# Adjacency GNN on one core: another order for the convolution taps, the second transposes and the opening's sums

## The chip, the cores and the metric

One core of a Trainium2 chip runs the kernel. The metric is the device time of one execution in microseconds (us). The kernel before has a median of 383.56 us over three runs (383.27 to 384.62).

## What is computed

The input is 32 graphs of 256 nodes with 128 features, and a 256 x 256 adjacency matrix for each. Two layers with a residual and a layer norm each:

```python
h = relu(bn1(conv1(x)));  x_conv = relu(bn2(conv2(h)) + x)          # conv2: 17 taps along the nodes
A = exp(-dist(x @ w_se)) * adj;  x_nmp = A @ relu(x @ w_msg)         # first product of a graph
y = GRU([x_conv, x_nmp], x);  x1 = layernorm(x + y)
h = (1 + eps) * x1 + adj @ x1                                        # second product of a graph
out = layernorm(x1 + relu(h @ W1 + b1) @ W2 + b2)
```

## The kernel before

The 32 graphs go in 8 groups of 4, a group in two pairs (index h). Every engine's instructions stand in an order written by hand in three functions: `prologue` (the opening, group 0's front part), `steady(s, u, front)` for the steps 1 to 7 and `last`. Steps 3 to 6 are a loop. In step s the back part of group s-1 (gates, first norm, product with the adjacency matrix, MLP, second norm) is interleaved with the middle part of group s (convolution, distances, product with A) and the front of group s+1 (`conv1`). Order between engines comes only from semaphores: each helper waits for the count of the stage that it reads and raises that of the stage that it writes. A wait holds up everything queued behind it on its engine.

The 17-tap convolution is done at seven points (HALF, ZERO, PLUS2, MINUS2, PLUS1, MINUS1, INF): input sums per point (`sv`), a short convolution of 4 or 5 taps on PE (L1367 in plain float32, L1314 as three products of high and low parts), and sums of the outputs on DVE into `usum` (L972 `u_sum`, L982 `pair2_sum`, L990 and L991 `pair2_add`, L995 `pair1_sum`, L1003 `pair1_add`, L1008 `inf_add`). High parts (`xh`, `sth`, `wh`, `nmph`) are rounded on ACT, low parts (`xl`, `stl`, `wl`, `nmpl`) are differences on DVE (L860, L1106). The weights' low parts are made in step 1 (`tap_low`) and the taps of each point in the opening (L1150).

Names that the change and the prediction touch:
- PE: `plain_taps`/`taps` (one point), `y_transpose(gb, h)` (L1479), `distances` (L1420), `aggregate` (the product with the adjacency matrix, L1428 into `back`), `nmp` (the product with A, L1428 into `front`), `mlp1`, `mlp2` (L1523), `conv1`.
- DVE: `y_stats` (L1044, L1048) and `y_apply` (L1066): first norm of a pair, with the root on POOL between them. `x_low` (L860, `xl`), `h_low` (L860, `nmpl` from `back`), `out_stats` (L1079, L1044, L1048): starts when `mlp2` is done.
- POOL: `rsqrt` (L543), `mask` (L564, `amat`, four in a step), `add_b2` (L558), `add_diagonal` (L577), and in step 1 alone `x_low1` (L569), which makes the low part of group 1's x.
- ACT: `h1_out` (L665), `minus2_out` (L678), `minus1_out` (L685), `exps` (L694).

A group counts two low parts of x on one semaphore, and group 1's are POOL's. So `x_low` has a wait for group 2 alone:

```python
if isinstance(g, int) and g == 2:
    wait(dve, XL_READY, 1, 2)
```

## Time and profile before

| | |
|---|---|
| median of three runs | 383.56 us (383.27 to 384.62) |
| the profiled execution | 383.36 us, of which 381.6 us are its span |
| busy PE, DVE, ACT, POOL | 95%, 85%, 61%, 56% of the span |
| granted TensorE clock | 0.996 on average |
| one loop step | 44.0 us, eight groups |

The span is the time between the first and the last instruction of the profiled execution. A row of the timeline gives the start and the duration in us, the engine, the line of the kernel, the operation, what it writes from what it reads, the count of merged instructions, and in brackets how long the engine had been idle and what ended that. The same tile name stands for all of its buffers.

### The profile page before, as it was taken

Reading aid. Unit: us, or ns where it says so; the run is one execution under the profiler, and the core shown is the slowest. Engines: PE = TensorE matmul, PEld = TensorE weight load, DVE = VectorE, ACT = ScalarE, POOL = GpSimd, SP = SyncE. Lnnn points to the kernel's source line nnn. Section 1 sums busy time; section 2 is a strip of 40 time slices with the busy share of each in tenths; the row PEclk is TensorE's granted clock in tenths of the full one; section 3 lists DMA queues with packets and bytes.
Section 4 is the critical chain, followed back from the end, with each engine's and each line's share of the span. In section 5 each row is a group of like instructions: output and inputs, shape, how many; then the busy total and the mean of one; then the engine's idle time right before and its main releaser. Section 6 shows DMA issues by size and latency. Waiting matters only on the chain.

```text
span 381.6 us, 6424 instructions
## 1 busy us (share of the span) xinstructions
PE 363.7 (95%) x2150; PEld 315.6 (83%) x2150; DVE 323.0 (85%) x674; ACT 232.3 (61%) x436; POOL 215.0 (56%) x190
## 2 busy tenths in 40 slices
PE   7998998899999999999999999999999999999994
PEld 4776778599898888989888998989888998988973
DVE  4999989998699986999689986999779986995584
ACT  3463665555767376673875657674676648555765
POOL 3135344946349753697437863497536973296362
PEclk9999999999999999999999999999999999999998
DMA  5700004200013010130110300130101301000002
GB/s 196 267 3 0 0 3 165 83 29 28 29 55 112 0 58 1 55 112 2 56 33 26 108 27 29 55 110 0 55 0 55 110 2 55 3 1 2 0 29 82
DMA packets 8135, 19.39 MB, mean 51 GB/s; under 512 B 688, under 2 KB 5168, under 8 KB 7088
## 3 DMA queue, kind: packets, MB, share of 16 engines
q1 hardware_dynamic: 7536, 18.17, 13.9%
q10 hardware_dynamic: 576, 0.92, 0.7%
q8 instruction: 13, 0.21, 0.2%
q14 instruction: 10, 0.08, 0.1%
HBM read 14.90 MB, written 4.19 MB: 50 GB/s over the span
## 4 chain that ended last, share of the span: by engine, by line
PE 60%; DVE 27%; issue 5%; ACT 2%; POOL 2%; DMA 2%; SPq 0%; DVEq 0%; ACTq 0%; POOLq 0%
PE back L1314 24%; PE conv L1314 16%; PE back L1428 5%; PE back L1523 3%; DVE stats L1044 3%; PE conv L1367 3%; DVE stl L860 3%; PE front L1400 2%; PE front L1428 2%; DVE tail L1079 2%; POOL rstd L543 2%; DMA xv<-in_x_dram 2%; DVE xn L1066 2%; DVE nmpl L860 1%; DVE wl L1106 1%
## 5 line engine op out<-in xcount | busy, mean ns | idle before, releaser
L1314 PE MATMUL conv<-sth,wh 128*128 128x256 f32 x207 | 62.4, 301 | 2.8 <-DVE stl L860 2.2
L1314 PE MATMUL conv<-sth,wl 128*128 128x256 f32 x207 | 58.9, 285 | 0.0
L1314 PE MATMUL conv<-stl,wh 128*128 128x256 f32 x207 | 58.8, 284 | 0.0
L543 POOL TENSOR_TENSOR rstd<-rstd,small 128x4 f32<-128x4 f32 (+1 forms) x34 | 38.3, 1127 | 34.2 <-DVE rstd L1048 33.7
L564 POOL TENSOR_TENSOR amat<-amat,adjT 128x512 f32<-128x512 f32 x32 | 49.4, 1576 | 9.6 <-ACT amat L694 9.6
L548 POOL TENSOR_TENSOR xw<-xw,xv 128x512 f32<-128x512 f32 (+1 forms) x17 | 21.7, 1279 | 48.0 <-ACT xw L718 48.0
L1314 PEld LDWEIGHTS conv<-sth,wh 128*128 128x128 f32 x207 | 39.0, 189 | 5.4 <-issue 1.6
L1314 PEld LDWEIGHTS conv<-stl,wh 128*128 128x128 f32 x207 | 39.0, 189 | 0.1
L1314 PEld LDWEIGHTS conv<-sth,wl 128*128 128x128 f32 x207 | 39.0, 189 | 0.0
L650 ACT ACTIVATE sth<-sv 128x272 fp32r<-128x272 f32 (+1 forms) x33 | 17.2, 522 | 34.2 <-DVE sv L888 22.2
L577 POOL TENSOR_TENSOR adjT<-adjT,diag 128x256 f32<-128x256 f32 x32 | 28.4, 916 | 6.1 <-DVE msg L934 6.1
L735 ACT ACTIVATE tail<-tail,shift,rstd 128x128 f32<-128x128 f32 x60 | 24.1, 481 | 11.2 <-DVE shift L1101 11.2
L1428 PE MATMUL front<-amat,msg 128*128 128x256 f32 x128 | 29.1, 379 | 0.0
L1428 PE MATMUL back<-adjT,xn 128*128 128x256 f32 x120 | 28.2, 387 | 0.8 <-DVE xn L1066 0.8
L558 POOL TENSOR_TENSOR tail<-xn,later_w 128x512 f32<-128x512 f32 x15 | 27.3, 1823 | 1.8 <-DVE xn L1066 1.4
L742 ACT ACTIVATE tail<-back,first_w 128x512 f32<-128x512 f32 (+1 forms) x30 | 20.4, 683 | 11.4 <-PE back L1314 11.4
L1523 PEld LDWEIGHTS back<-later_w,tail 128*128 128x128 f32 x224 | 26.2, 192 | 0.6
L1523 PE MATMUL back<-later_w,tail 128*128 128x128 f32 x224 | 26.3, 275 | 0.0
L1428 PEld LDWEIGHTS back<-adjT,xn 128*128 128x128 f32 x120 | 22.0, 190 | 5.2 <-DVE xn L1066 1.5
L1428 PEld LDWEIGHTS front<-amat,msg 128*128 128x128 f32 x128 | 23.8, 190 | 2.9
L528 POOL TENSOR_TENSOR sv<-vv 128x272 f32<-128x272 f32 x7 | 8.3, 1187 | 30.3 <-DVE vv L915 30.3
L1003 DVE TENSOR_TENSOR usum<-usum,pm 128x512 f32<-128x512 f32 x16 | 23.7, 1518 | 0.1
(240 smaller groups left out, 1036.4 us busy)
## 6 DMA issues: line engine op xcount, KB each, us to landing
adjT<-in_adj_dram SPq DMA_DIRECT2D x8, 1024.0 KB, 4.9
out_dram<-tail SPq DMA_DIRECT2D x15, 256.0 KB, 2.2
xv<-in_x_dram SPq DMA_DIRECT2D x7, 512.0 KB, 3.3
tail<-in_conv_dram ACTq DMA_DIRECT2D x3, 256.0 KB, 4.5
gbuf<-in_gates_dram SPq DMA_DIRECT2D x1, 576.0 KB, 8.2
xv<-in_x_dram SPq DMA_DIRECT2D x2, 256.0 KB, 5.3
tail<-in_conv_dram SPq DMA_DIRECT2D x1, 320.0 KB, 5.0
later_w<-in_later_dram SPq DMA_DIRECT2D x1, 320.0 KB, 5.3
```

The source lines that it names most:

```text
L543: done(pool.tensor_tensor(rstd[:, k, v, q], rstd[:, k, v, q], minus_half[:, q], ALU.pow), RSTD[k])
L548: done(pool.tensor_tensor(xw[:, h, part(c)], xw[:, h, part(c)], xv[u][:, part_cols(h, c)], ALU.mult), XWX_READY)
L558: done(pool.tensor_tensor(out_tile(h, c)[:, q, :], xn[:, h, q, :], b2bc.unsqueeze(1).to_broadcast([P, len(part_blocks(c)), D]), ALU.add), ...
L564: done(pool.tensor_tensor(amat[:, b, :, :], amat[:, b, :, :], adjT[u][:, b, :, :], ALU.mult), A_READY)
L577: done(pool.tensor_tensor(dg, dg, diag[:, :].unsqueeze(1).to_broadcast([P, PAR, P]), ALU.add), ADJE_READY)
L650: done(act.activation(dst, src, ACT.Copy), name)
L735: last = act.activation(o[:, q, :], o[:, q, :], ACT.Identity, bias=shift[:, v, q:q + 1], scale=rstd[:, 1, v, q:q + 1])
L742: done(act.activation(hid[:, h, f, part(c)], bank("hid", h, c, f), ACT.Relu, bias=vec[:, B1 + f:B1 + f + 1]), HID_READY)
L1003: done(dve.tensor_tensor(a, a, p1, ALU.add), PRE_READY)
L1314: ins = pe.matmul(bank, a, b, start=first and k == 0, stop=last and k == len(todo) - 1)
L1428: ins = pe.matmul(tile[:, k * N:(k + 1) * N], lhs(b, rm), rhs(b, rm), start=rm == 0, stop=rm == PAR - 1)
L1523: ins = pe.matmul(tile[:, k * P:(k + 1) * P], hid[:, h, f, q * P:(q + 1) * P], w2[:, f, :], start=f == 0, stop=f == 1)
```

## The change

Only orders change, no instruction is added or removed. The opening: on ACT `h1_out` of group 0 goes ahead of the second high part of x, and `minus2_out(0)` ahead of two of the exponentials. On DVE `u_sum(0)` and `pair2_sum(0)` go ahead of the stream and the taps at -1, and the low part of x goes behind the output sums. On PE the product `nmp(0, 0)` goes ahead of the taps at -1. On POOL the first two `add_diagonal` wait for `inf_add` and no longer for a rounded product. In the steps: on PE the taps at -1 stand directly behind those at 1, the second `y_transpose` behind them with the distances, and INF ahead of both `aggregate`. In step 1 `mlp2(gb, 0)` goes ahead of `conv1`. DVE follows: `pair2_sum` and the low part of INF's stream ahead of the second `y_stats`, one `x_low` ahead of the second `y_apply` and one behind it, and `pair2_add` behind both `h_low`.

```diff
--- before.py
+++ after.py
@@ -595,7 +595,7 @@
                 streams2(1)
                 pool.wait_ge(mlp_loaded, 16)
                 pool.wait_ge(diag_ready, 1)
-                wait(pool, NH_READY, 0, 1)
+                wait(pool, PRE_READY, 0, 3)
                 add_diagonal(0, 0, 0)
                 add_diagonal(0, 0, 1)
                 wait(pool, MSUM_READY, 1, 1)
@@ -755,12 +755,12 @@
                 act.activation(wh[:, 0, :], c1raw, ACT.Copy).then_inc(w_high, 1)
                 act.wait_ge(x_pair0_loaded, 16)
                 high(xh[0][:, cols(0)], xv[0][:, cols(0)], XH_READY)
-                wait(act, X_LOADED, 0, 16)
-                high(xh[0][:, cols(1)], xv[0][:, cols(1)], XH_READY)
                 act.wait_ge(pads_zeroed, 1)
                 act.wait_ge(bn_ready, 1)
                 h1_out(0, 0)
                 h1_out(0, 1)
+                wait(act, X_LOADED, 0, 16)
+                high(xh[0][:, cols(1)], xv[0][:, cols(1)], XH_READY)
                 act.wait_ge(conv2_loaded, 64)
                 x_high(1, 1)
                 for k in range(3):
@@ -774,11 +774,11 @@
                 h1_out(1, 0, True)
                 exps(0, 0)
                 exps(0, 1)
-                h1_out(1, 1, True)
+                act.wait_ge(bn_ready, 3)
+                minus2_out(0)
                 exps(0, 2)
                 exps(0, 3)
-                act.wait_ge(bn_ready, 3)
-                minus2_out(0)
+                h1_out(1, 1, True)
                 act.wait_ge(tap_sums, 11)
                 tap_high(PLUS1)
                 minus1_out(0)
@@ -1175,12 +1175,12 @@
                 taps_step(even, w0, 1.0, w2)
                 taps_step(minus1, w1, 1.0, w3)
                 taps_step(plus1, even, 1.0, minus1)
+                dve.wait_ge(tap_sums, steps[0])
+                u_sum(0, 0)
+                pair2_sum(0)
                 first_stream1(MINUS1, ALU.subtract)
                 taps_step(minus1, minus1, -1.0, even)
                 dve.wait_ge(tap_sums, steps[0])
-                u_sum(0, 0)
-                x_low(0, 0, 1)
-                pair2_sum(0)
                 first_diffs(1)
                 half_stream(1)
                 zero_stream(1)
@@ -1191,9 +1191,10 @@
                 pair1_add(0, 1)
                 inf_add(0)
                 nmp_low(0, 0)
+                nmp_low(0, 1)
                 xconv_low(0, 0)
-                nmp_low(0, 1)
                 w_low_part(wl[:, S_GATE:S_GATE + 9, :], graw, wh[:, S_GATE:S_GATE + 9, :], w_count("gates"))
+                x_low(0, 0, 1)
                 tap_low(PLUS1)
                 xconv_low(0, 1)
 
@@ -1207,16 +1208,15 @@
                 if first:
                     stream_low(gm, 2)
                 reset(gb, 0)
+                add_input(gb, 0)
                 if first:
                     tap_low(MINUS2)
-                add_input(gb, 0)
                 gates_end(gb, 0)
                 stream_low(gm, 3)
                 if first:
                     tap_low(ZERO)
                     reset(gb, 1)
                     tap_low(MINUS1)
-                    inf_stream(gm)
                 else:
                     inf_stream(gm)
                     u_sum(gm, u)
@@ -1224,28 +1224,31 @@
                 add_input(gb, 1)
                 y_stats(gb, 0)
                 gates_end(gb, 1)
+                if first:
+                    inf_stream(gm)
                 y_apply(gb, 0)
-                y_stats(gb, 1)
                 pair2_sum(gm)
-                y_apply(gb, 1)
-                stream_low(gm, 4)
                 if first:
                     tap_low(INF)
+                stream_low(gm, 4)
+                y_stats(gb, 1)
+                if front:
+                    x_low(gf, 1 - u, 0)
+                y_apply(gb, 1)
+                if first:
                     w_low_part(w1l[:, :], w1raw, w1h[:, :], w_count("w1"))
                     h_low(gb, 0)
                     u_sum(gm, u)
+                    h_low(gb, 1)
+                    pair1_sum(gm)
+                    x_low(gf, 1 - u, 1)
                 else:
-                    pair2_add(gm)
+                    if front:
+                        x_low(gf, 1 - u, 1)
                     h_low(gb, 0)
                     pair1_sum(gm)
-                h_low(gb, 1)
-                if first:
-                    pair1_sum(gm)
-                if front:
-                    x_low(gf, 1 - u, 0)
-                    x_low(gf, 1 - u, 1)
-                if first:
-                    pair2_add(gm)
+                    h_low(gb, 1)
+                pair2_add(gm)
                 pair1_add(gm, 0)
                 pair1_add(gm, 1)
                 if second:
@@ -1551,8 +1554,8 @@
                 for b in range(GB):
                     distances(0, b)
                 plain_taps(0, PLUS1)
+                nmp(0, 0)
                 plain_taps(0, MINUS1)
-                nmp(0, 0)
                 plain_taps(1, HALF)
                 nmp(0, 1)
                 plain_taps(1, ZERO)
@@ -1580,28 +1583,31 @@
                     pe.wait_ge(w_low, w_count(MINUS2))
                 taps(gm, MINUS2)
                 taps(gm, PLUS1)
-                y_transpose(gb, 1)
                 if first:
                     pe.wait_ge(w_low, w_count(MINUS1))
                 taps(gm, MINUS1)
+                y_transpose(gb, 1)
                 distances(gm, 0)
                 distances(gm, 1)
+                if first:
+                    pe.wait_ge(w_low, w_count(INF))
+                taps(gm, INF)
                 aggregate(gb, ub, 0)
                 aggregate(gb, ub, 1)
                 distances(gm, 2)
                 distances(gm, 3)
                 if first:
-                    pe.wait_ge(w_low, w_count(INF))
-                taps(gm, INF)
-                if first:
                     pe.wait_ge(w_low, w_count("w1"))
                     pe.wait_ge(mlp_loaded, 16)
                 mlp1(gb, 0)
                 mlp1(gb, 1)
+                if first:
+                    mlp2(gb, 0)
                 if front:
                     conv1(gf, ub, 0)
                     conv1(gf, ub, 1)
-                mlp2(gb, 0)
+                if not first:
+                    mlp2(gb, 0)
                 if front:
                     mlp2(gb, 1)
                 nmp(gm, 0)
```

DVE in the opening, from the taps at 1 to the first instruction of group 1 (L972, L976: `u_sum`; L982: `pair2_sum`; L882 and the last L1150: stream and taps at -1; `xl`: `x_low`; L875: `first_diffs(1)`):

```order
 L1150 SCALAR_TENSOR_TENSOR gbuf<-adjT 128x640
+L972 SCALAR_TENSOR_TENSOR usum<-conv,first_w,xv 128x4x64 x4
+L976 SCALAR_TENSOR_TENSOR usum<-conv,first_w,usum 128x4x64
+L982 SCALAR_TENSOR_TENSOR pm<-conv,first_w,pm 128x4x64 x2
 L882 TENSOR_TENSOR sv<-vv 128x272
 L1150 SCALAR_TENSOR_TENSOR adjT<-adjT 128x640
-L972 SCALAR_TENSOR_TENSOR usum<-conv,first_w,xv 128x4x64 x4
-L976 SCALAR_TENSOR_TENSOR usum<-conv,first_w,usum 128x4x64
-L860 TENSOR_TENSOR xl<-xv,xh 128x512
-L982 SCALAR_TENSOR_TENSOR pm<-conv,first_w,pm 128x4x64 x2
 L875 TENSOR_TENSOR av<-h 128x4x2x68
```

The output sums now run before the stream and the taps at -1, and `x_low` has left this stretch.

DVE in step 1 with the changed order, from `tap_low(INF)` through the second pair's norm (the waits stand in brackets; `xl_ready` counts the low parts of x, `rstd1_ready` the roots of the first norm):

```order
L1106 TENSOR_TENSOR wl<-tail,wh 128x512 [waits w_high]
L860 TENSOR_TENSOR stl<-sv,sth 128x272 [waits streams_high_ready]
L1044 BN_STATS stats<-back 128x6 [waits y_full]
L1044 BN_STATS stats<-back 128x6
L1048 TENSOR_SCALAR rstd<-stats 128x4 [waits stats1_ready]
L860 TENSOR_TENSOR xl<-xv,xh 128x512 [waits xl_ready,xh_ready]
L1066 TENSOR_SCALAR xn<-back,stats,rstd 128x128 [waits rstd1_ready]
L1066 TENSOR_SCALAR xn<-back,stats,rstd 128x128 x3
L1106 TENSOR_TENSOR w1l<-later_w,w1h 128x256 [waits w_high]
```

Before, both `xl` instructions stood behind `pair1_sum`, well behind `w1l`. Now the first stands between the statistics (L1048) and the normalisation (L1066) of the second pair.

DVE in step 2, from the second pair's statistics to `pair1_add` (the loop steps read the same), before:

```order
L1048 TENSOR_SCALAR rstd<-stats 128x4
L982 SCALAR_TENSOR_TENSOR pm<-conv,first_w,pm 128x4x64 x2
L1066 TENSOR_SCALAR xn<-back,stats,rstd 128x128 x4
L860 TENSOR_TENSOR stl<-sv,sth 128x272
L990 TENSOR_TENSOR usum<-usum,pm 128x512
L991 SCALAR_TENSOR_TENSOR usum<-pm,usum 128x512
L860 TENSOR_TENSOR nmpl<-back,nmph 128x512
L995 SCALAR_TENSOR_TENSOR pm<-conv,first_w,pm 128x512
L860 TENSOR_TENSOR nmpl<-back,nmph 128x512
L860 TENSOR_TENSOR xl<-xv,xh 128x512 x2
L1003 TENSOR_TENSOR usum<-usum,pm 128x4x128 x2
```

and with the change:

```order
L1048 TENSOR_SCALAR rstd<-stats 128x4
L860 TENSOR_TENSOR xl<-xv,xh 128x512
L1066 TENSOR_SCALAR xn<-back,stats,rstd 128x128 x4
L860 TENSOR_TENSOR xl<-xv,xh 128x512
L860 TENSOR_TENSOR nmpl<-back,nmph 128x512
L995 SCALAR_TENSOR_TENSOR pm<-conv,first_w,pm 128x512
L860 TENSOR_TENSOR nmpl<-back,nmph 128x512
L990 TENSOR_TENSOR usum<-usum,pm 128x512
L991 SCALAR_TENSOR_TENSOR usum<-pm,usum 128x512
L1003 TENSOR_TENSOR usum<-usum,pm 128x4x128 x2
```

The two `x_low` have moved forward, and `pair2_add` (L990, L991) has taken their place directly ahead of `pair1_add` (L1003).

## Rows read from the trace of the kernel before

**Rows 1.** Windows by stage: length, busy us (count) of PE, PEld, DVE, ACT, POOL.
```profile
0.00:45.35 45.35, 39.25 (x172) 30.26 (x173) 38.66 (x78) 22.34 (x41) 14.73 (x24) 1.00 0.29 98
45.35:89.90 44.55, 41.58 (x238) 35.17 (x237) 42.00 (x83) 24.97 (x45) 27.36 (x23) 1.00 0.16 60
89.90:135.63 45.73, 44.34 (x269) 38.79 (x267) 40.49 (x83) 28.53 (x54) 28.71 (x23) 1.00 0.14 47
...
179.65:223.75 44.10, 43.83 (x271) 38.92 (x272) 38.33 (x80) 28.33 (x53) 27.44 (x23) 1.00 0.14 49
```

**Rows 2.** Timeline of PE, opening and step 1, rows with idle time before them.
```profile
34.81 2.44 PE L1367 MATMUL conv<-sv,first_w 128*128 128x256 f32 x10 [1.51 <-DVE sv L888]
...
41.39 2.41 PE L1367 MATMUL conv<-sv,first_w 128*128 128x256 f32 x10 [0.68 <-issue]
...
63.94 0.63 PE L1479 MATMUL back<-ident_w,gbuf 128*128 128x128 f32 x4 [1.06 <-DVE gbuf L1037]
...
76.40 0.47 PE L1314 MATMUL back<-nmph,w1h 128*128 128x512 f32 x1 [0.93 <-DVE nmpl L860]
```

**Rows 3.** Timeline of DVE in the opening.
```profile
27.13 1.89 DVE L1150 SCALAR_TENSOR_TENSOR adjT<-adjT 128x640 f32<-128x640 f32 x1
...
31.02 0.92 DVE L860 TENSOR_TENSOR xl<-xv,xh 128x512 fp32r<-128x512 f32 x1
...
38.40 2.29 DVE L1003 TENSOR_TENSOR usum<-usum,pm 128x512 f32<-128x512 f32 x2
```

**Rows 4.** Timeline of POOL in the opening.
```profile
25.52 5.87 POOL L564 TENSOR_TENSOR amat<-amat,adjT 128x512 f32<-128x512 f32 x4 [9.60 <-ACT amat L694]
...
38.29 1.85 POOL L577 TENSOR_TENSOR adjT<-adjT,diag 128x256 f32<-128x256 f32 x2
```

**Rows 5.** Timeline of DVE in step 1.
```profile
65.98 0.17 DVE L1048 TENSOR_SCALAR rstd<-stats 128x4 f32<-128x4 f32 x1
...
67.27 1.37 DVE L1066 TENSOR_SCALAR xn<-back,stats,rstd 128x128 f32<-128x128 f32 x4 [0.34 <-POOL rstd L543]
...
71.60 1.50 DVE L1106 TENSOR_TENSOR w1l<-later_w,w1h 128x256 fp32r<-128x256 f32 x1
...
79.42 1.29 DVE L1003 TENSOR_TENSOR usum<-usum,pm 128x512 f32<-128x512 f32 x2
```

**Rows 6.** Timeline of POOL in step 1.
```profile
66.23 1.01 POOL L543 TENSOR_TENSOR rstd<-rstd,small 128x4 f32<-128x4 f32 x1 [1.10 <-DVE rstd L1048]
67.20 1.28 POOL L569 TENSOR_TENSOR xl<-xv,xh 128x512 fp32r<-128x512 f32 x1
...
80.86 1.34 POOL L519 TENSOR_TENSOR av<-h 128x544 f32<-128x544 f32 x1 [4.12 <-ACT h L665]
```

**Rows 7.** Timeline of DVE in a loop step, from 205 us.
```profile
205.00 0.68 DVE L990 TENSOR_TENSOR usum<-usum,pm 128x512 f32<-128x512 f32 x1
...
208.17 2.76 DVE L860 TENSOR_TENSOR xl<-xv,xh 128x512 fp32r<-128x512 f32 x2
210.86 3.47 DVE L1003 TENSOR_TENSOR usum<-usum,pm 128x512 f32<-128x512 f32 x2
214.98 0.69 DVE L1079 TENSOR_TENSOR tail<-back,tail 128x512 f32<-128x512 f32 x1 [0.66 <-PE back L1523]
```

**Rows 8.** Timeline of POOL in the same loop step.
```profile
204.82 2.62 POOL L558 TENSOR_TENSOR tail<-xn,later_w 128x512 f32<-128x512 f32 x1 [0.24 <-DVE xn L1066]
207.38 6.40 POOL L564 TENSOR_TENSOR amat<-amat,adjT 128x512 f32<-128x512 f32 x4
```

**Rows 9.** Timeline of PE in the same loop step and at its end.
```profile
200.75 0.37 PE L1314 MATMUL conv<-sth,wh 128*128 128x256 f32 x1
200.96 0.28 PE L1314 MATMUL conv<-stl,wh 128*128 128x256 f32 x1
201.07 0.28 PE L1314 MATMUL conv<-sth,wl 128*128 128x256 f32 x1
...
223.75 0.38 PE L1314 MATMUL conv<-sth,wh 128*128 128x256 f32 x1 [0.27 <-DVE stl L860]
```

## The prediction

> **What bounds the kernel now.** I read the windows by stage first [rows 1]. In a loop step PE is busy 43.83 of 44.10 us, in the opening 39.25 of 45.35, in step 1 41.58 of 44.55, in step 2 44.34 of 45.73. A stage here ends where PE begins the taps at 2, except the opening, which ends where the gates begin. So an order of work can win at most 6.1 us in the opening, 3.0 in step 1, 1.4 in step 2 and 0.3 in each of the four loop steps. DVE has 38 to 42 busy us in the same windows and is the second bound.
>
> The timeline of PE then shows who ends the idle time [rows 2]: DVE's half stream of group 1 (1.51 us at 34.81), `inf_add` on DVE (0.68 at 41.39, which the view calls issue; the taps at 2 of group 1 wait for it), the second gate output ahead of the second `y_transpose` in step 1 (1.06 at 63.94), the second `h_low` (0.93 at 76.40). At the end of a loop step it is a low part of a stream (0.27 at 223.75, [rows 9]). All of these are DVE's. So DVE is read next, beside POOL.
>
> **DVE and POOL hold each other up.** `pair1_add` takes 1.29 us for two instructions where POOL is idle [rows 5], 2.29 beside `add_diagonal` [rows 3, 4] and 3.47 beside four masks [rows 7, 8]. So an instruction of 0.65 waits for about one POOL instruction. The reverse is seen too: `add_b2` takes 2.62 us where DVE runs `pair2_add` beside it, and `pair2_add` keeps its 0.68 [rows 7, 8]. Which of two waits is decided by who comes first.
>
> **The opening: -1.7 us.** The low part of x (0.92) leaves DVE's way to group 1's streams [rows 3]. The first two `add_diagonal` now start behind `inf_add`, so `pair1_add` should cost 1.29 instead of 2.29, 1.0 less [rows 3, 4, 5]. Against that, the taps at -1 (1.89 under a mask [rows 3]) now stand behind `u_sum` and `pair2_sum`: done at 29.0 before, they are done when the masks let them, which run from 25.52 to 31.39 [rows 4]. The taps' 640 elements take some 0.8 us by `pair1_add`'s 0.65 for 512, just ahead of the last mask's end or behind it: 31.0 to 32.2, 31.7 taken. PE uses the gap for `nmp(0, 0)`, and from 31.7 it has work without a hole: the taps at -1 (ten instructions like the half stream's, 2.2 us) and what it did from 34.81 to 45.35 less 0.68 idle, 9.8 us [rows 1, 2]. The gates would start at 43.7 instead of 45.35: -1.7. At best all 2.5 us of PE's idle time after 29 go away, at worst only `x_low`'s 0.9. The earlier `h1_out` costs and brings nothing: DVE wins some tenths by it, which end in the same wait for the masks.
>
> **Step 1: +1.6 us.** The second `y_transpose` no longer leaves 1.06 of idle time in front of it. But the new order has a wait that the diff doesn't show as such: `x_low` of group 2 waits for POOL's low part of group 1, and now stands between the second pair's statistics and its normalisation. POOL does the root first (1.01), then that low part (1.28), and only then may DVE go on [rows 6]. Before, the statistics ended at 66.15 and the normalisation began at 67.27, 1.12 later [rows 5]. Now: 1.01 + 1.28 + two handovers of 0.05 + `x_low` itself 0.65 = 3.0, so 1.9 us more on DVE, and 3.2 if POOL's next instruction, `add_b2`, gets in ahead of `x_low` (2.62 less the 1.3 of `pair2_add` [rows 7, 8]). DVE's work up to the second `h_low` is the end of PE's idle time at 76.40, so the delay goes to PE. What gives it back in part is `w1l`, which waits for less POOL work (1.50 before [rows 5], 0.4 at best). There is a second brake: `mlp2(0, 0)` goes ahead of `conv1`, which moves `h1_out` and POOL's `token_diffs` of group 2 (80.86, [rows 6]) about 1.8 us back against the MLP, and DVE's streams of group 2 need them. Bounds of what is given back: 0.7 (`w1l` and half of the wait hidden) to 2.7. I take 1.6, nearly all that the opening wins, because both brakes act on the same stretch.
>
> **Step 2: +0.65 us, the loop steps: +0.6 us together.** PE has the same work, so only what DVE finishes late counts. It counts from `out_stats`, which starts when `mlp2` ends (214.98) after 0.66 of idle time [rows 7]. The second `h_low` ended at 208.17 [rows 7]; INF's twelve instructions now lie ahead of the second `aggregate`, 12 x 0.12 [rows 9] = 1.5 us, so it ends at 209.7. Behind it stand four instructions of 0.65 that read and write SBUF: `pair2_add` has changed places with the two `x_low`. The masks: 6.40 us less three waits of 0.6 are 1.15 each [rows 8]; they begin at about 208.1, because `add_b2` comes 1.5 later and is held up less. Alternating, DVE's four end at 215.3, or at 214.7 if the phase is kinder: 0 to 0.3 us late, 0.15 taken, over four loop steps 0.6. If each waits longest, 0.6 per step. In step 2 two weights' low parts follow `pair1_add` and the idle time is gone already (1.4 us of PE idle time, [rows 1]), so all of the later end counts: 0.65, between 0 and 1.2. Step 7 has no `x_low` and no wait at its end: nothing.
>
> **PE's changes of kind: -0.6 us.** The first tap behind a `y_transpose` takes 0.21 us to the next one, the second 0.11 [rows 9]. The taps at -1 behind those at 1 save that 0.09, seven times. At most twice that, if the `distances` behind it save as much, at least nothing: no row shows `distances` behind a transpose.
>
> **The sum.** -1.7 + 1.6 + 0.65 + 0.6 - 0.6 = +0.55 on the profiled execution's 383.36 us: 383.9. The median of the runs is 0.2 above it, so I say 384.0 us. Against the median that is +0.1%; 0.5%, 1.9 us, is about what can be told from no change. The ends added up: -2.5 + 0.7 - 1.2 gives 380.4, -0.9 + 2.7 + 1.2 + 2.4 gives 388.8.
>
> **Rivals.** First, **the opening's gain stays**: POOL's low part is done by the time DVE asks, or DVE catches up because it has fewer waits. For it: DVE's idle 0.34 ahead of the normalisation goes [rows 5], and step 1 loses the 1.06 [rows 2]. Against it: POOL's low part stands behind a root that needs the very statistics ahead of `x_low`. Time: 383.36 - 1.7 - 1.06 - 0.6 = 380.0. Chance 0.15.
>
> Second, **the masks hold DVE in every step**: all four instructions behind the second `h_low` wait for POOL, and `out_stats` starts late. It decides where `pair1_add` ends more than 0.66 us later than before [rows 7]; from there every tenth is one of PE's. With 3.47 / 2 = 1.74 for each of the four [rows 7], from 209.7 to 216.7, less one that finds POOL done (1.1) and half of another: 215.9 to 216, 0.9 late. Four loop steps 3.6, step 2 1.4, the rest as forecast (-1.7 + 1.6 - 0.6): +4.3, so 387.7. Chance 0.24. For it: `pair2_add` never ran beside masks in a step before. Against it: the first two masks now run while DVE waits for `h_low`. The Trainium skill (SBUF — State Buffer, section "SBUF: two separate sides") has it that a DVE instruction with two SBUF inputs and a GpSimd instruction that reads SBUF exclude each other for a whole instruction, the first one there winning. By that rule moving two such instructions under the masks costs what this rival says; the 2.62 and the 3.47 agree with it.
>
> Third, that **the change doesn't do what it says**, since PE is without a hole in the loop and its groups only change places: then only the opening and step 1 speak, between 382.7 (-1.7 + 1.6 - 0.6) and 384.4 (-1.7 + 2.7). That lies within the forecast's case, which has 0.61.
>
> **How the numbers follow.** Forecast 0.61, nearly all of it within 0.5%. Faster by over 0.5% (under 381.6): most of the first rival, 0.14. Slower (over 385.5): the second and the forecast's upper tail, 0.25. Same 0.61. The range from 381.0 to 387.2 cuts the outer part of either rival, a tenth at each end.
>
> **What would show it.** Right: the gates start at 43 to 44.5 us; DVE idles 1 us or more ahead of `xl` in step 1, ended by POOL's L569; the second `h_low` of step 1 is about where it was; `pair2_add` takes 1 to 1.8 us for an instruction; PE's gap ahead of the taps at 2 in the loop is 0.2 to 0.6. Wrong: no idle time ahead of that `xl`, and step 2 beginning 2 us or more earlier (first rival); loop steps of over 44.6 us (second); or an opening that isn't shorter, because the taps at -1 come later than 32.2.

## The result and the profile after

The changed kernel takes 394.3 us (median of 6 runs, 392.87 to 395.28), the kernel before 383.5 (6 runs, 383.27 to 384.62): a ratio of 1.028, 95% interval 1.0264 to 1.0296. It is slower by 10.8 us where 0.5 was forecast, and the time lies above the range. The profiled execution has a span of 392.4 us against 381.6.

The windows by stage of the kernel after, cut as in [rows 1] (the opening ends where the gates begin, every step where PE begins the taps at 2; then length, busy us and count of PE, PEld, DVE, ACT, POOL, and the granted clock):

```profile
0.00:43.14 43.14, 38.87 (x172) 30.40 (x173) 36.76 (x77) 22.25 (x41) 13.64 (x24) 1.00 0.30 103
43.14:91.32 48.18, 43.99 (x239) 37.16 (x237) 43.35 (x83) 24.11 (x45) 26.26 (x23) 0.93 0.15 56
91.32:139.36 48.04, 44.67 (x266) 38.73 (x267) 41.95 (x83) 28.60 (x54) 28.05 (x24) 1.00 0.12 44
...
184.22:229.14 44.92, 44.24 (x271) 38.70 (x272) 38.04 (x80) 28.09 (x53) 26.85 (x23) 1.00 0.15 48
...
318.88:392.40 73.52, 65.01 (x393) 56.89 (x393) 50.53 (x118) 42.84 (x85) 33.72 (x34) 0.96 0.07 22
```

The opening is 2.2 us shorter than in [rows 1]. Step 1 is 3.6 longer, step 2 2.3, a loop step 0.8, and the stretch from step 7 to the end takes 73.5 us where it took 69.8 (311.78 to 381.6). The loss is in every step, and in step 1 (0.93, before 1.00) and at the end (0.96, before 0.98) the clock column is lower too.

**Step 1.** PE in the kernel after, by its timeline (start, length, engine, line, operation, idle time before it):

```profile
66.29 0.55 PE L1317 MATMUL conv<-sth,wh 128*128 128x256 f32 x1 [3.18 <-DVE stl L860]
66.64 0.41 PE L1317 MATMUL conv<-stl,wh 128*128 128x256 f32 x1
66.86 0.41 PE L1317 MATMUL conv<-sth,wl 128*128 128x256 f32 x1
...
68.99 5.51 PE L1431 MATMUL back<-adjT,xn 128*128 128x256 f32 x16
```

And DVE in the same stretch:

```profile
65.17 0.67 DVE L1106 TENSOR_TENSOR wl<-tail,wh 128x512 fp32r<-128x512 f32 x1
65.77 0.42 DVE L860 TENSOR_TENSOR stl<-sv,sth 128x272 fp32r<-128x272 f32 x1
...
69.50 1.67 DVE L860 TENSOR_TENSOR xl<-xv,xh 128x512 fp32r<-128x512 f32 x1 [2.43 <-POOL xl L569]
```

The wait that the prediction expected is there: `x_low` stands 2.43 us and takes 1.67, and the normalisation begins 2.9 us later behind the statistics than before (71.09 - 67.07 against 1.12, [rows 5]), near the worse of its two cases. But PE shows a larger hole that it did not expect: 3.18 us ahead of INF, ended by the stream's low part (65.77), which DVE reaches only behind `pair2_sum` and INF's weight (65.17). And behind the hole PE runs slowly. A tap followed the one before by 0.11 us in [rows 9] and follows by 0.22 here, and the two aggregates (16 matmuls) take 5.51 us, where they took 3.94 in the kernel before. The windows behind the hole show the clock that was granted:

```profile
66.20:69.00 2.80, 2.71 (x13) 2.74 (x14) 0.84 (x3) 1.53 (x4) 1.85 (x2) 0.50 0.00 0
69.00:72.00 3.00, 3.00 (x9) 2.35 (x8) 2.50 (x4) 0.00 (x0) 1.62 (x2) 0.50 0.00 0
72.00:75.00 3.00, 2.89 (x15) 1.87 (x14) 2.72 (x8) 1.06 (x2) 2.47 (x2) 0.99 0.00 0
```

0.50 is the lower of the two levels, 1.2 GHz. It was granted from the hole's end to about 72 us.

**A loop step.** DVE of the kernel after, by the timeline:

```profile
208.34 0.69 DVE L860 TENSOR_TENSOR xl<-xv,xh 128x512 fp32r<-128x512 f32 x1
209.93 1.37 DVE L1066 TENSOR_SCALAR xn<-back,stats,rstd 128x128 f32<-128x128 f32 x4 [0.90 <-POOL rstd L543]
...
214.62 1.44 DVE L990 TENSOR_TENSOR usum<-usum,pm 128x512 f32<-128x512 f32 x1
215.99 1.77 DVE L991 SCALAR_TENSOR_TENSOR usum<-pm,usum 128x512 f32<-128x512 f32 x1
217.86 2.18 DVE L1003 TENSOR_TENSOR usum<-usum,pm 128x512 f32<-128x512 f32 x2
219.97 0.68 DVE L1079 TENSOR_TENSOR tail<-back,tail 128x512 f32<-128x512 f32 x1
...
221.48 1.09 DVE L1048 TENSOR_SCALAR rstd<-stats 128x4 f32<-128x4 f32 x1
```

POOL beside it:

```profile
208.48 1.42 POOL L543 TENSOR_TENSOR rstd<-rstd,small 128x4 f32<-128x4 f32 x1 [3.93 <-DVE rstd L1048]
...
212.99 5.90 POOL L564 TENSOR_TENSOR amat<-amat,adjT 128x512 f32<-128x512 f32 x4
219.49 1.76 POOL L519 TENSOR_TENSOR av<-h 128x544 f32<-128x544 f32 x1 [0.59 <-ACT h L665]
221.21 1.33 POOL L521 TENSOR_TENSOR av<-h 128x544 f32<-128x544 f32 x1
```

And the load of PE's weights for the second aggregate:

```profile
211.35 1.59 PEld L1431 LDWEIGHTS back<-adjT,xn 128*128 128x128 f32 x8 [0.53 <-DVE xn L1066]
```

`pair2_add` (L990, L991) now takes 1.44 and 1.77 us beside the masks, where it took 0.68 each [rows 7]: what the second rival described. `pair1_add` ends 35.8 us after the taps at 2 began (220.04 - 184.22), in the kernel before 34.7 (214.33 - 179.65, [rows 7]), and the 0.66 of idle time ahead of `out_stats` is gone. Two more things are late, though. The second normalisation ends 27.1 us after the taps at 2 (211.30 - 184.22), before it was 25.1, and in spite of INF in front of it the second aggregate waits 0.53 us. And the variance of `out_stats` (L1048, a 128x4 instruction) takes 1.09 us beside POOL's `token_diffs`, in the kernel before 0.68. Which of the three sets the step, one profile doesn't tell. The experiments go into it, and the rows of all of them together give an answer (below, "What all runs share").

**Step 7 and the last group.** PE ahead of the last gates:

```profile
358.23 0.47 PE L1317 MATMUL back<-xh,wh 128*128 128x512 f32 x1 [2.00 <-DVE nmpl L860]
```

The windows around them:

```profile
358.00:360.00 2.00, 1.77 (x5) 1.46 (x6) 1.30 (x3) 0.00 (x0) 2.00 (x4) 0.69 0.04 8
360.00:362.00 2.00, 2.00 (x6) 1.60 (x5) 0.00 (x0) 0.03 (x1) 1.35 (x2) 0.50 0.00 0
```

The gates wait 2.00 us for `nmp_low`, which stands behind `pair2_add`, `pair1_add`, `inf_add` and `out_stats` on DVE. Then they run at 0.50 again, up to about 362 us. The prediction had put this stage at nothing.

### The profile page after: what moved, and what is told of

Read it like the earlier page. It is cut to its first block, busy times and chain, and to the rows that moved or that the text cites. A ratio compares the mean times of both kernels' runs of the same rounds, so it can differ in the third digit from the quotient of the medians.

```text
span 392.4 us, 6424 instructions
## 1 busy us (share of the span) xinstructions
PE 369.1 (94%) x2150; PEld 318.2 (81%) x2150; DVE 324.1 (83%) x674; ACT 230.6 (59%) x436; POOL 208.4 (53%) x190
## 4 chain that ended last, share of the span: by engine, by line
DVE 37%; PE 34%; issue 15%; POOL 5%; ACT 4%; DMA 2%; SPq 0%; DVEq 0%; ACTq 0%; POOLq 0%
PE back L1317 14%; PE conv L1317 6%; PE back L1431 4%; POOL rstd L543 4%; DVE stats L1044 4%; PE conv L1370 3%; DVE stl L860 3%; DVE usum L991 3%; DVE xn L1066 3%; DMA xv<-in_x_dram 2%; DVE gbuf L1029 2%; DVE usum L990 2%; PE front L1403 2%; DVE wl L1106 2%; DVE tail L1079 2%
## 5 line engine op out<-in xcount | busy, mean ns | idle before, releaser
L543 POOL TENSOR_TENSOR rstd<-rstd,small 128x4 f32<-128x4 f32 (+1 forms) x34 | 39.9, 1174 | 50.5 <-DVE rstd L1048 50.1
L564 POOL TENSOR_TENSOR amat<-amat,adjT 128x512 f32<-128x512 f32 x32 | 46.1, 1472 | 9.8 <-ACT amat L694 9.8
L1431 PE MATMUL back<-adjT,xn 128*128 128x256 f32 x120 | 30.4, 400 | 1.6 <-DVE xn L1066 1.2
L1431 PE MATMUL front<-amat,msg 128*128 128x256 f32 x128 | 29.1, 379 | 0.0
L1431 PEld LDWEIGHTS back<-adjT,xn 128*128 128x128 f32 x120 | 22.8, 199 | 7.3 <-DVE xn L1066 3.3
L650 ACT ACTIVATE nmph<-back 128x512 fp32r<-128x512 f32 (+1 forms) x16 | 9.2, 572 | 29.5 <-PE back L1431 29.5
L1066 DVE TENSOR_SCALAR xn<-back,stats,rstd 128x128 f32<-128x128 f32 x60 | 20.5, 403 | 6.3 <-POOL rstd L543 5.6
L558 POOL TENSOR_TENSOR tail<-xn,later_w 128x512 f32<-128x512 f32 x15 | 21.0, 1402 | 3.7 <-DVE xn L1066 3.4
```

The costliest lines, as they stand in the source:

```text
L543: done(pool.tensor_tensor(rstd[:, k, v, q], rstd[:, k, v, q], minus_half[:, q], ALU.pow), RSTD[k])
L558: done(pool.tensor_tensor(out_tile(h, c)[:, q, :], xn[:, h, q, :], b2bc.unsqueeze(1).to_broadcast([P, len(part_blocks(c)), D]), ALU.add), ...
L564: done(pool.tensor_tensor(amat[:, b, :, :], amat[:, b, :, :], adjT[u][:, b, :, :], ALU.mult), A_READY)
L650: done(act.activation(dst, src, ACT.Copy), name)
L1066: last = dve.tensor_scalar(xn[:, h, q, :], src(q, q + 1), stats[:, 0, v, q, 1:2], rstd[:, 0, v, q:q + 1], ALU.subtract, ALU.mult)
L1431: ins = pe.matmul(tile[:, k * N:(k + 1) * N], lhs(b, rm), rhs(b, rm), start=rm == 0, stop=rm == PAR - 1)
```

## The experiments

All were compared with the kernel before on the same chip. The table is worked out from the timelines: a step runs from the first `messages` instruction of its group on PE to that of the next group, and the last column but one from that of step 7 to the end of the span. Steps 3 to 6 are a mean. The steps are those of the profiled execution, and they add up to its span; the time, a median, is 0.2 to 2.9 us above that span.

```
kernel                     to step 1  step 1  step 2  3 to 6   end    time
before                       43.64    48.43   45.49   44.04   67.9   383.5
after                        41.43    52.13   47.73   44.88   71.6   394.3
e3 opening alone             41.08    49.29   45.48   44.05   67.8   382.5
e4 steps alone               44.01    51.66   48.31   44.88   70.0   395.1
e1 pair2_add back            42.47    52.00   46.25   45.05   68.9   390.8
e2 INF back                  42.71    54.90   46.40   45.97   70.1   399.2
e5 x_low behind norm.        41.27    52.28   47.83   44.94   71.7   394.6
e6 DVE's old tail            41.95    52.17   47.84   44.95   68.9   392.4
e7 mlp2 back in step 1       41.16    51.43   47.77   44.88   71.6   393.4
e8 transposes back           41.55    53.60   47.88   44.47   71.5   394.4
e9 transposes alone          41.55    49.27   47.08   45.55   69.4   391.6
e10 step 1 as before         43.10    49.28   47.74   44.88   71.6   391.5
e11 opening, late nmp_low    41.38    49.28   45.05   43.65   67.8   380.2
e12 INF between aggregates   42.55    53.60   48.31   44.88   70.0   395.2
e13 e8 and e1 together       41.38    51.92   45.80   44.59   68.6   389.0
e14 remainder, late nmp_low  41.14    49.31   45.38   44.21   68.6   383.4
e15 e13, masks first         41.26    52.69   48.99   49.38   69.1   411.3
```

The column "to step 1" also holds how soon the first work of all starts (9.1 to 10.9 us from run to run). Without that it is 34.1 us in the kernel before and e4, which have the old opening, and 32.0 to 32.4 in all others.

### The two halves of the change

e3 takes the opening's part of the diff into the kernel before; e4 takes the same part out of the kernel after.

> The kernel before with the change's opening alone (POOL's wait, ACT's, DVE's and PE's prologues). Theory: the opening's 2.2 us (gates at 43.14 instead of 45.35) is a gain of its own that step 1 passes on: 383.5 - 2.2 = 381.3 us. Rival (step 1 gives it back, because its streams' low parts and weights are ready no earlier and x of group 1 or its weights' low parts hold PE): 382.5 to 383.5 us.

382.48 us against 383.33, ratio 0.998 (0.9969 to 0.9992). In the profile the messages of step 1 start 2.6 us earlier, 0.5 of which is an earlier start of the first work (9.08 against 9.56). Step 1 gives 0.9 back: PE waits 0.57 us there for a gate's output of ACT's (at 55.43), and later for the same low parts as before. That leaves 1.2, and the times say 0.85: a small gain, and the rival's numbers (382.5 to 383.5) rather than the theory's 381.3.

> The changed kernel with the opening of the kernel before: the changes of the steps alone. Theory: the two parts add up, 394.3 + 2.2 = 396.5 us, with step 1 at 48 us, steps 3 to 6 at 44.9 and PE's gaps of 3 us in step 1 and 2 us ahead of the last gates. Rival (step 1's loss is the opening's gain given back, since DVE's list up to INF's stream takes equally long whenever the gates begin): 394 to 395 us, step 1 at 46 us.

395.08 us: 0.8 more than the kernel after, not 2.2. The loss is in the steps. Step 1 takes 51.66 us behind the old opening too, so its loss isn't the opening's gain given back. The halves don't simply add up: the end of e4 takes 1.6 us less than that of the kernel after, with a clock that stays at 1.00 there (last section).

### Step 1

e10 gives step 1 the lists of the kernel before on DVE and PE and leaves the other steps as changed.

> The changed kernel with the order of the kernel before on DVE and PE in step 1 alone (opening and steps 2 to 7 as changed). Theory (step 1's loss is its own: INF ahead of the aggregates waits 3.18 us for its stream's low part, PE's clock is granted at half behind that gap, and the aggregates wait for x_low's late normalisation): step 1 takes 49.3 us from messages to messages as in the kernel with the opening alone (52.1 in the changed kernel), PE's clock is 1.00 there: 394.3 - 2.8 = 391.5 us. Rival (part of it comes back in step 2, whose DVE is full as well): 392.5 to 393.5 us.

Step 1 is 49.28 us, as with the opening alone, and 391.48 in all: 2.8 us of the loss belong to step 1's order, and step 2 takes none of it over (47.74). Which part of that order is it? e5 moves the first `x_low`:

```diff
                 y_stats(gb, 1)
-                if front:
-                    x_low(gf, 1 - u, 0)
                 y_apply(gb, 1)
...
                     pair1_sum(gm)
+                    x_low(gf, 1 - u, 0)
                     x_low(gf, 1 - u, 1)
...
```

The lines shown at the end are those of step 1. In steps 2 to 7 it goes directly behind `y_apply`.

> The changed kernel with the first x_low taken out from between the second pair's statistics and its normalisation (behind the normalisation in steps 2 to 7, behind pair1_sum in step 1); nothing else. Theory X (x_low in that place holds the normalisation, by itself in step 1, and in the loop by slowing POOL's root beside it from 1.02 to 1.42 us): in steps 3 to 6 the root is 1.02 us again, the second aggregate no longer waits (0.53 us before), and a step takes 44.4 to 44.6 instead of 44.9 us; in step 1 the 2.43 us of idle time ahead of xl and the 1.67 of xl itself go from DVE's way, and step 1 is 1.5 to 2.5 us shorter. Together 394.3 - 1.6 - 2 = 390.5 us. Rival (the pair2_add behind the h_lows is what sets out_stats, and step 1 waits for the streams of group 2): the loop stays at 44.9, step 1 gains less than 0.7 us, about 393.5 us.

394.57 us, step 1 at 52.28 and the loop at 44.94: nothing, in either. The wait is gone and nothing is won, because DVE now idles in front of the first `h_low` instead. The timeline of DVE in e5:

```profile
69.32 1.43 DVE L1106 TENSOR_TENSOR w1l<-later_w,w1h 128x256 fp32r<-128x256 f32 x1
73.05 0.69 DVE L860 TENSOR_TENSOR nmpl<-back,nmph 128x512 fp32r<-128x512 f32 x1 [2.30 <-ACT nmph L650]
```

The aggregate that this `h_low` reads runs at half clock (16 matmuls in 5.28 us) and is what comes last. So the wait that the prediction had costed stood beside one that it had not seen, and taking away the first alone brings nothing. e2 takes the hidden part from the other side: INF goes behind both aggregates, as before.

```diff
-                if first:
-                    pe.wait_ge(w_low, w_count(INF))
-                taps(gm, INF)
                 aggregate(gb, ub, 0)
                 aggregate(gb, ub, 1)
                 distances(gm, 2)
                 distances(gm, 3)
+                if first:
+                    pe.wait_ge(w_low, w_count(INF))
+                taps(gm, INF)
```

> The changed kernel with INF put back behind both aggregates on PE in every step; DVE's order as changed. Theory A (pair2_add's place alone costs): the four instructions behind the second h_low still alternate with the masks, and as both the h_lows and the masks come 1.5 us earlier, out_stats is late no more than before: it recovers in this kernel as well, 44.0 to 44.3 us in steps 3 to 6; then lateness is the sum of two moves and either alone is free. Theory B (INF's place costs): the same in the loop. They part in step 1: there INF waits for its stream's low part, which was the 3.18 us gap at 66.29; behind the aggregates that gap should be gone and step 1 fall from 48.2 to about 45.5, unless x_low's wait of 2.43 us on DVE only moves it to the MLP (46.5). All together 394.3 - 3 (loop) - 2 (step 2) - 2 (step 1) - 2 (step 7) = 385 us; if pair2_add's place costs by itself, the loop steps stay at 44.6 or more and the time at about 390.

399.21 us, the opposite of what I had expected, in the loop too. PE's timeline of e2, in step 1:

```profile
73.78 3.56 PE L1431 MATMUL back<-adjT,xn 128*128 128x256 f32 x8 [5.96 <-DVE xn L1066]
```

and in a loop step:

```profile
215.21 1.99 PE L1431 MATMUL back<-adjT,xn 128*128 128x256 f32 x8 [1.60 <-DVE xn L1066]
```

Without INF in front, the second aggregate waits 5.96 us for the normalisation in step 1 and 1.6 in each loop step. So in the loop INF ahead of the aggregates is a cover: it hides a normalisation that the rest of the change has made late. e12 tries the middle, INF between the aggregates:

```diff
                 aggregate(gb, ub, 0)
+                if first:
+                    pe.wait_ge(w_low, w_count(INF))
+                taps(gm, INF)
                 aggregate(gb, ub, 1)
```

> The changed kernel with INF between the two aggregates of every step instead of ahead of both. Theory (in step 1 the gap of 3.18 us in front of INF and the half clock behind it cost most of the 3 us; in the loop it is DVE that is late, in whatever order PE goes): in step 1 the first aggregate runs in the gap, INF waits at most 1.3 us, the granted clock stays at 1.00, and step 1 takes 49.5 to 50.5 us from messages to messages instead of 52.1; the loop stays at 44.8 to 45: 394.3 - 2 = 392.3 us. Rival (the half clock is no matter, x_low's wait of 2.43 us on DVE then holds the second aggregate): step 1 at 51.5 to 52.5, 394 us.

395.22 us. The loop is the same to 0.01 us, and step 1 is 1.5 us longer. There the hole moves to the second aggregate, by PE's timeline of e12:

```profile
73.61 3.67 PE L1431 MATMUL back<-adjT,xn 128*128 128x256 f32 x8 [4.46 <-DVE xn L1066]
```

and by its windows the clock falls behind this hole:

```profile
72.00:75.00 3.00, 1.40 (x3) 1.17 (x4) 3.00 (x9) 0.00 (x0) 1.37 (x2) 0.77 0.00 0
75.00:78.00 3.00, 3.00 (x12) 1.96 (x11) 1.50 (x5) 0.69 (x2) 2.47 (x3) 0.66 0.00 0
```

So the run doesn't price the half clock by itself; e8 and e13 below do. e7 undoes the "second brake":

```diff
-                if first:
-                    mlp2(gb, 0)
...
-                if not first:
-                    mlp2(gb, 0)
+                mlp2(gb, 0)
```

> The changed kernel with mlp2 of the first pair behind conv1 in step 1 as well, as before. Theory (second brake: mlp2 ahead of conv1 delays ACT's h1_out of group 2, POOL's token_diffs and with it the half stream by up to 1.9 us): PE's conv1, h1_out and token_diffs come 1 to 1.5 us earlier and step 1 ends 0.8 to 1.5 us earlier: 393 us. Rival (out_stats, which waits for that mlp2, stands ahead of the half stream on DVE and moves back as far): no gain, 394 to 395 us.

393.42 us, step 1 at 51.43: 0.7 us, a little under the expectation. That brake is real.

### The loop

e1 is the test of the second rival:

```diff
                         x_low(gf, 1 - u, 1)
+                    pair2_add(gm)
                     h_low(gb, 0)
                     pair1_sum(gm)
                     h_low(gb, 1)
-                pair2_add(gm)
+                if first:
+                    pair2_add(gm)
```

> The changed kernel with pair2_add put back ahead of the two h_lows in steps 2 to 7 (step 1 as changed). Theory A (the place of pair2_add is what costs: it stands behind the second h_low and alternates with the masks): of the +10.8 us of the changed kernel's profile, steps 3 to 6 lose their +0.83 each (44.0 to 44.2 us again), step 2 its excess of 2.3, and step 7 with the last group its 3.7, since inf_add and both nmp_low come 2 us or more earlier and PE's gap of 2.00 us ahead of the last gates goes, with the half clock behind it; step 1 stays at 48.2. About 394.3 - 3.3 - 2.0 - 3.4 = 385.6 us. Theory B (INF ahead of the aggregates moves everything behind it, whatever DVE's order): the steps stay at 44.6 to 44.9, about 392 us. Theory C (DVE pays ahead of the h_lows instead): pair2_add beside add_b2 delays the first h_low, PE waits in front of mlp1, 388 to 390 us.

390.77 us (ratio 1.0191, 1.0174 to 1.0208). Theory A holds for step 2 (46.25, 1.5 us less) and for the end (68.9, 2.7 less), and falls for the loop: 45.05 us, no better. There DVE now waits 2.29 us ahead of `out_stats`, and the step is no shorter. By POOL's rows the second `add_b2` now stands beside `pair2_add` and takes 2.87 us (1.65 in the kernel after), the masks end 1.2 us later in the step, and `token_diffs` starts only when they end. e6 gives DVE its old tail in steps 2 to 7 (in step 1 both `x_low` go behind `pair1_sum`):

```diff
                 y_stats(gb, 1)
-                if front:
-                    x_low(gf, 1 - u, 0)
                 y_apply(gb, 1)
...
-                    if front:
-                        x_low(gf, 1 - u, 1)
+                    pair2_add(gm)
                     h_low(gb, 0)
                     pair1_sum(gm)
                     h_low(gb, 1)
+                    if front:
+                        x_low(gf, 1 - u, 0)
+                        x_low(gf, 1 - u, 1)
...
```

> DVE's order of the kernel before from the normalisation on in steps 2 to 7 (pair2_add ahead of the h_lows, both x_low behind them), in step 1 the two x_low behind pair1_sum; the rest of the changed kernel. If x_low's place and pair2_add's place are each a cost, this is the sum: the loop at 44.1 to 44.3 us, step 2 at 46, the last group without its gap of 2 us, step 1 at 46: 383.5 + 2 = 385.5 us. If what costs in the loop is INF ahead of the aggregates with its stream's low part ahead of the second pair's statistics, whatever stands behind them, the loop stays at 44.7 or more, about 388 us.

392.43 us, the loop at 44.95, the second of the two cases. PE is on time there (`mlp1` begins 29.1 us after the taps at 2, 214.04 - 184.95, before 29.2), and the step is no shorter. In the timeline of DVE in e6 the masks hold `x_low` and `pair1_add` up to `out_stats`, because the second `h_low` ends 30.0 us after the taps at 2, where it was 28.5 in [rows 7]:

```profile
214.96 2.50 DVE L860 TENSOR_TENSOR xl<-xv,xh 128x512 fp32r<-128x512 f32 x2
217.38 3.47 DVE L1003 TENSOR_TENSOR usum<-usum,pm 128x512 f32<-128x512 f32 x2
220.77 0.68 DVE L1079 TENSOR_TENSOR tail<-back,tail 128x512 f32<-128x512 f32 x1
```

POOL's `token_diffs` starts directly behind the masks, and with those adds of DVE's beside it the first takes 1.79 us instead of 1.34, by POOL's timeline of e6:

```profile
220.25 1.79 POOL L519 TENSOR_TENSOR av<-h 128x544 f32<-128x544 f32 x1
```

e8 puts the second transposes back ahead of the taps at -1, and e9 makes that one move alone, on top of the opening:

```diff
                 taps(gm, PLUS1)
+                y_transpose(gb, 1)
...
                 taps(gm, MINUS1)
-                y_transpose(gb, 1)
```

> The changed kernel with the second y_transpose of every step back ahead of the taps at -1. Theory (the second transposes set the chain statistics, root, normalisation, second aggregate, which the loop waits for): the statistics of the second pair start 0.35 us earlier (DVE is free then), the wait of the second aggregate falls from 0.53 to 0.2, a loop step takes 44.5 to 44.6 instead of 44.9, and 0.1 per step comes back for the taps' first instruction: 392.5 to 393.5 us; in step 1 PE waits about 1 us in front of the second y_transpose again, and the gap of 3.18 us ahead of INF is 1 us shorter. Rival (the transposes' place is harmless): 394.3 to 395 us, the loop at 44.9 or 45.

394.44 us. The loop gets its 0.4 us (44.47). Step 1 takes 1.5 us more, but not by this move: e13 below has the same order in step 1 and takes 51.92 there. In both, PE is without work for 1.88 us ahead of INF, and the second aggregate begins with the normalisation, 31.1 us after the messages. In e8 it then runs at the lower clock (0.50 from 73 to 76 us, 8 matmuls in 3.64 us). In e13 the lower clock came earlier (0.56 from 67 to 70), ahead of that wait, and the same 8 take 1.99. So here the half clock by itself costs 1.7 us, or nothing where a wait hides it.

> The kernel before with the change's opening, and of the steps' changes only one: the second y_transpose of every step behind the taps at -1. Theory M (the moves hold each other up: the late transposes need INF ahead of the aggregates as a cover, INF needs its stream's low part early, and that delays the second pair's statistics): alone, the transposes make the normalisation of the second pair 1.5 us later and the second aggregate waits about 1.2 us for it; the h_lows and the masks come later, and a loop step takes 45 us or more against 44.05 in the kernel with the opening alone: 382.5 + 6 = 388 us. Rival (the place of the transposes is harmless, or a small gain as forecast, 0.09 us per step): 382 to 382.5 us, the loop at 44.0.

391.57 us, ratio 1.0213 (1.0199 to 1.0228): 9 us more than with the opening alone, from a move that the prediction counted as a gain of 0.6. Step 1 is as long as with the opening alone (49.27). The row of PE is the one expected, once in every step:

```profile
208.26 1.99 PE L1429 MATMUL back<-adjT,xn 128*128 128x256 f32 x8 [1.18 <-DVE xn L1066]
```

So the late transposes make the second aggregate wait 1.2 us for its normalisation and a loop step 1.5 us longer, and INF in front is what hides this (e2 takes it away, and the wait is back). The rest of the loss should then go with `pair2_add` and the transposes both back:

> The changed kernel with two parts back: the second y_transpose ahead of the taps at -1, and pair2_add ahead of the h_lows in steps 2 to 7. Alone, the first took 0.42 us from a loop step, the second nothing. Theory (two lists end at out_stats, PE's by way of the late transposes and DVE's by way of pair2_add under the masks, each late by about half a us, and POOL's token_diffs behind both; only taking both away lets the step go): a loop step at 44.0 to 44.15 us, 0.3 to 0.4 less than with the transposes back alone; step 2 from messages to messages at 45.5 to 46.3; the last group as with pair2_add back alone, 63.2; step 1 at 53.6 as with the transposes back alone. Together 394.4 - 1.4 - 1.8 - 2.7 = 388.5 us. Rival (INF ahead of the aggregates has a price of its own, since the second h_low and the masks still come 1.5 us later): the loop at 44.4 to 44.5, about 390 us.

389.02 us, the loop at 44.59: the theory fell, and the rival's numbers (44.4 to 44.5, about 390) are near. PE begins its first `mlp1` 29.2 us after the taps at 2 as in the kernel before, and DVE waits. DVE in e13:

```profile
217.13 0.69 DVE L1079 TENSOR_TENSOR tail<-back,tail 128x512 f32<-128x512 f32 x1 [2.29 <-PE back L1528]
...
218.66 1.17 DVE L1048 TENSOR_SCALAR rstd<-stats 128x4 f32<-128x4 f32 x1
```

and POOL:

```profile
211.28 5.93 POOL L564 TENSOR_TENSOR amat<-amat,adjT 128x512 f32<-128x512 f32 x4
217.17 1.34 POOL L519 TENSOR_TENSOR av<-h 128x544 f32<-128x544 f32 x1
218.47 1.33 POOL L521 TENSOR_TENSOR av<-h 128x544 f32<-128x544 f32 x1
```

The same place in the kernel before, POOL's and DVE's timeline (a loop step whose taps at 2 begin at 179.65):

```profile
214.51 1.34 POOL L519 TENSOR_TENSOR av<-h 128x544 f32<-128x544 f32 x1 [0.74 <-ACT h L665]
215.82 1.33 POOL L521 TENSOR_TENSOR av<-h 128x544 f32<-128x544 f32 x1
...
216.50 0.68 DVE L1048 TENSOR_SCALAR rstd<-stats 128x4 f32<-128x4 f32 x1
...
221.83 0.17 DVE L1048 TENSOR_SCALAR rstd<-stats 128x4 f32<-128x4 f32 x1
```

What is late is POOL. Its second `add_b2` starts behind the late normalisation and takes 2.88 us beside `pair2_add`, the masks follow, and `token_diffs` starts the moment they end, 35.4 us after the taps at 2 (217.17 - 181.74). In the kernel before, it waited 0.74 us for ACT and started at 34.9 (214.51 - 179.65). The variance on DVE (L1048) stands beside it and takes 1.17 instead of 0.68 us. That is 0.5 us on a list of DVE's that runs without a pause from `out_stats` to the low part for the taps at 2, and the step is longer by 0.54. e15 shortens POOL's list by taking the first two masks ahead of the second `add_b2`:

```diff
                 add_b2(gb, 0)
+                mask(gm, u, 0)
+                mask(gm, u, 1)
                 add_b2(gb, 1)
-                for b in range(GB):
-                    mask(gm, u, b)
+                mask(gm, u, 2)
+                mask(gm, u, 3)
```

> The kernel with transposes and pair2_add back (loop steps at 44.57 us), and on POOL the first two masks ahead of the second add_b2 in steps 1 to 7. Theory (a third list: in that kernel neither PE nor DVE is late at out_stats, where DVE idles 2.29 us, but POOL goes from the masks into token_diffs without a pause, 35.4 us after the taps at 2 instead of 34.9, and out_norm's variance on DVE then waits 1.17 instead of 0.68 for token_diffs): the first two masks run while POOL waited for the normalisation or beside the second add_b2's place, the masks end 1 us or more earlier, L1048 takes 0.68 or less again and a loop step 44.0 to 44.15 us, about 387 us in all. Rival (POOL's order is no matter, INF's place costs through PE or DVE in a way not yet seen): the loop stays at 44.5 to 44.6, 389 us.

411.32 us. The row that the theory speaks of is as expected, L1048 at 0.68. But the step is 4.8 us longer, by the price of masks beside DVE. DVE's timeline of e15:

```profile
216.33 1.70 DVE L862 TENSOR_TENSOR xl<-xv,xh 128x512 fp32r<-128x512 f32 x1
217.96 1.75 DVE L992 TENSOR_TENSOR usum<-usum,pm 128x512 f32<-128x512 f32 x1
219.63 1.75 DVE L993 SCALAR_TENSOR_TENSOR usum<-pm,usum 128x512 f32<-128x512 f32 x1
...
232.46 0.68 DVE L1050 TENSOR_SCALAR rstd<-stats 128x4 f32<-128x4 f32 x1
```

and by the windows of e15 from the MLP's start:

```profile
222.13:224.13 2.00, 2.00 (x5) 1.61 (x6) 2.00 (x3) 0.34 (x1) 1.62 (x2) 0.50 0.39 164
224.13:226.13 2.00, 2.00 (x7) 1.52 (x6) 0.77 (x2) 1.03 (x2) 0.00 (x0) 0.50 0.00 0
```

`x_low` and `pair2_add`, now in front of the first `h_low`, wait for a mask each (1.7 us instead of 0.68), the MLP starts 3.19 us late, and behind that hole the clock is at 0.50 for 4 us and more. So e15 doesn't show what the loop would take with a shorter list of POOL's. Nor does its L1048 stand free of POOL: in the kernel before it takes 0.68 at this place and 0.17 in the second `out_stats` (the last row above), so 0.68 holds a wait already.

**What all runs share.** In each of the four loop steps of all 17 kernels traced here, L1048 ends 0.01 to 0.04 us behind the second `token_diffs` (in the kernel before at 217.18 and 217.15, after at 222.57 and 222.54, in e13 at 219.83 and 219.80). The messages of the next step begin 8.4 to 8.5 us behind that end, and 8.0 to 8.1 in e11 and e14 below, which take `nmp_low` out of the way. So by the rows the end of POOL's `token_diffs` sets the length of a loop step in every run, that of the kernel before included. From the messages of its step it ends at 35.6 us there and at 36.4 in the kernel after, which is the 0.8 that a step loses. Half of that is a later start: 0.4 us, with ACT's `h`, which follows PE's `mlp1` and `conv1` (0.3 and 0.4 later). Half is the first `token_diffs` itself, 1.76 instead of 1.34 beside DVE's late `pair1_add` and `out_stats`. In e1, e5, e6, e13 and e14 the start waits for the masks instead. No run moves `token_diffs` alone, so that this is the cause is read from the rows.

### A version that beats both

The kernel before already had that list of DVE's behind L1048, and PE's 0.27 of idle time at its end [rows 9]. e11 is e3 with one instruction moved out of it:

```diff
-                    nmp_low(gm, 0)
                     inf_add(gm)
                     stream_low(gf, 2)
+                    nmp_low(gm, 0)
                     nmp_low(gm, 1)
```

> The kernel with the opening alone, and nmp_low of the first pair behind inf_add and the low part of the stream of the taps at 2 (both on DVE, steps 1 to 6). Theory (already before the change a loop step is set by PE up to the first mlp2 and then by DVE's unbroken list from out_stats to the low part that the taps at 2 wait for): 0.6 us less ahead of that low part takes away PE's idle 0.27 us per step and 0.6 in step 2: steps 3 to 6 at 43.8 to 43.85, step 2 at 45.0, and 382.5 - 1.6 = 380.9 us. Rival (ACT's high part of that stream, not DVE's list, comes last, or nmp_low's delay holds the next messages): steps at 44.0 to 44.1 or more, 382 to 383 us.

380.24 us, ratio 0.9917 (0.9902 to 0.9932): faster than both kernels, by 3.1 us against the kernel before and 2.2 against e3. The window of a loop step:

```profile
177.42:221.11 43.69, 43.69 (x273) 38.91 (x272) 38.77 (x80) 28.13 (x54) 27.01 (x23) 1.00 0.14 49
```

PE is busy in all of it, and a step is 0.4 us shorter. All of that is the hole at the step's end: up to the last taps PE's rows in e3 and e11 agree to 0.01 us from the messages on. The tap behind the hole started 0.54 us after the one ahead of it (223.21 and 223.75 in the kernel before), where 0.12 is usual; the 0.27 of idle time is only the part in which nothing ran. e14 has the same, and what is left of the change once step 1, the transposes and `pair2_add` are as before:

> What is left of the change when the costly parts are out: its opening, and in steps 2 to 7 INF ahead of the aggregates, the stream's low part early and both x_low ahead of the h_lows; step 1 in the order of before, transposes and pair2_add in steps 2 to 7 as before, and nmp_low of the first pair behind the low part for the taps at 2 in every step. If these parts cost nothing, it ties with the kernel that has the opening and the late nmp_low alone (380.2 us, loop steps at 43.65 without a hole on PE); if INF's place costs, the loop is at 43.8 to 44 and the time at 381.5 to 382.5 us. Lower than 380 only if a step other than the loop's gains.

383.37 us, the loop at 44.21 against 43.65, more than either case expected. The parts that are left (INF in front with its low part early, `x_low` ahead of the normalisation; no run separates them) cost 0.56 us per loop step, and DVE's rows of e14 show where: 2.30 us of idle time ahead of `out_stats` and L1048 at 1.17 again.

```profile
213.47 0.69 DVE L1079 TENSOR_TENSOR tail<-back,tail 128x512 f32<-128x512 f32 x1 [2.30 <-PE back L1610]
...
215.00 1.17 DVE L1048 TENSOR_SCALAR rstd<-stats 128x4 f32<-128x4 f32 x1
```

## Why the prediction was wrong

**The opening, -1.7.** Right in kind, and -2.2 by the windows. The taps at -1 were done at 31.23 in the kernel after (forecast 31.7), `pair1_add` took 1.29 us for two as forecast, and the gates start at 43.14. What the run's time keeps of it is 0.85 (e3).

**Step 1, +1.6.** This term was mis-sized, and its reason was half of it. "`x_low` of group 2 waits for POOL's low part" came as forecast, 2.43 us, but e5 took it away for nothing. The prediction did not ask when INF's stream is ready: DVE finishes that low part at 66.19, and PE, which has only `distances` left, is out of work at 63.11. INF moved to the front on PE, past the 16 matmuls of the aggregates and the last `distances`. On DVE its low part could not move as far, behind work without a pause from 56 to 66 us. The two waits end within 0.3 us of each other: `mlp1` begins 33.43 us after the messages in the kernel after, 33.20 in e5, 33.41 in e13, where the second aggregate starts with the normalisation at full clock, and 31.07 in e3. So by these rows either alone costs some 2 us, and no run takes away both and nothing else. With step 1 in its old order the 2.8 us go (e10); the rest of the 3.6 is what the opening's gain loses there (e3). The second brake was right, at 0.7 of the 2.8.

**The loop steps, +0.15 each.** The step that failed is "PE has the same work, so only what DVE finishes late counts", counted from `out_stats` and put at 0 to 0.3 us. The loop lost 0.83 per step. `out_stats` begins 0.4 us later in the step (219.97 - 184.22 against 214.98 - 179.65), and another 0.4 comes behind it, at L1048, which ends with POOL's `token_diffs`. POOL's list has no term in the prediction. The kernel before had three lists that end near the same place with little to spare: PE up to `conv1` and `mlp2` (0.27 at the step's end), DVE's adds (0.66 ahead of `out_stats`) and POOL's masks (0.74 ahead of `token_diffs`). The change makes the second normalisation 2.0 us later, and all three begin with it. I followed one list. e6 frees PE, e1 frees DVE, e13 frees both, and the step stays longer than before in each: in all three POOL's masks are late, and `token_diffs` starts when they end.

**The changes of kind, -0.6.** The saving was argued from 0.09 us at a tap. By PE's rows it isn't there: `distances` begins 23.11 us after the taps at 2 (207.33 - 184.22), before 23.09 (202.74 - 179.65). What the transposes delay was not followed either: e9 measures +1.5 us per loop step for that move alone.

**The second rival, 387.7 at 0.24.** Its condition came true: `pair1_add` ended 1.1 us later in the step, more than its 0.66. Its own sum doesn't give the 0.9 that it states: 216.7 less 1.1 is 215.6, 0.6 late, and half of another less makes it 0.1. By the rule of the Trainium skill (SBUF — State Buffer, section "SBUF: two separate sides") two such instructions exclude each other. The 1.44 and 1.77 for `pair2_add` beside the masks agree, and the 1.7 in e15. But where it was to cost most, in the loop, `pair2_add` back in its place brings nothing. It cost 1.5 us in step 2 and at the end, with the clock, 2.7 (e1).

**Step 7, nothing.** Wrong by 3.7. "Step 7 has no `x_low` and no wait at its end" overlooked that `inf_add` and both `nmp_low` stand behind `pair2_add` there, and that the last gates wait for them. 2.1 us are that wait and what follows. 1.6 are the half clock, by the difference of the kernel after (71.6) from e4 and e12 (70.0 each), where the same 2.00 us of idle time left the clock at 1.00.

**Step 2, +0.65.** It lost 2.3: its DVE list has two weights' low parts as well, so lateness counts in full, as the prediction said. The loss was over three times as large, and 1.5 of it is `pair2_add` (e1).

By the windows the parts make the whole: -2.2 + 3.6 + 2.3 + 3.4 + 3.7 = 10.8 us, the difference of the spans.

## What to carry to other kernels

When an operation moves, follow its result, not only its engine: list everything that begins with it on every engine and read how much each of these lists has to spare where they meet. The smallest slack counts, and removing one late list only shows the next. A stage that is full on one engine can still be set by another engine's unbroken list: look for the instruction in it that nobody waits for yet (here `nmp_low`, 0.6 us, which paid 2.2 us).

## What the runs showed that I had not expected

A hole in PE's work can cost its own length and a stretch at the lower clock behind it. After 3.18 us in step 1 the granted clock was 0.50 to about 72 us; after 2.66 us in step 2 of the same run it stayed at 1.00. In e4 and e12 the same hole in step 2 (2.67) was followed by 0.67 and 0.50, and step 2 is 0.6 us longer there. The 2.00 us ahead of the last gates (1.90 in e8) were followed by 0.50 in the kernel after, e5, e7, e8 and e10, and by 1.00 in e4 and e12: the same hole at the same place, with 1.6 us between them. What decides there was not settled.

POOL's smallest instructions are held as well: the root of 128x4 takes 1.01 us alone (e6, 209.21) and 1.42 in the kernel after (208.48) beside an `x_low` of DVE's that started 0.14 us before it.
